# A fused perceiver block: value copies, one gather and the last query tile change their engine or their place

## The reference

```python
# ctx_1024: (16, 1601, 512); 16 heads of 32
q = split_heads(layernorm(x) @ Wq); k = split_heads(ctx @ Wk); v = split_heads(ctx @ Wv)
attn = softmax(einsum('bhid,bhjd->bhij', q, k) * 32 ** -0.5)
x = x + merge_heads(einsum('bhij,bhjd->bhid', attn, v)) @ Wp + bp
x = x + self_attention(layernorm(x))
x = x + spikes(square(relu(layernorm(x) @ W_fc.T)) @ W_proj.T)
```

## Time and profile before

| | |
|---|---|
| timed runs | 1820.93, 1821.0, 1822.01 us; median 1821.0 |
| profiled execution | 1822.05 us, its span 1820.3 us |
| granted TensorE clock, mean | 0.999 of 2.4 GHz |
| TensorE busy | 1786.8 us, 98% of the span |
| VectorE / ScalarE / GpSimd busy | 1260.9 / 825.9 / 908.5 us |
| one turn of the batch loop | 88.7 us (first key tiles at 675.26 and 763.96) |

### The profile page before, as it was taken

How to read it: one execution, slowest core, us unless ns; L and a number is a source line. 1 busy time by engine, 2 the same in 40 slices (tenths; PEclk the granted TensorE clock), 3 DMA queues, 4 the chain that set the end, 5 groups by cost and what they waited for, 6 DMA issues and landing times. The chain is left out here.

```text
span 1820.3 us, 65817 instructions
## 1 busy us (share of the span) xinstructions
PE 1786.8 (98%) x28788; PEld 1560.4 (86%) x28788; DVE 1260.9 (69%) x1942; ACT 825.9 (45%) x982; POOL 908.5 (50%) x824
## 2 busy tenths in 40 slices
PE   9999999999999999999999999999999999999998
PEld 8979898979898989898989898988888877778887
DVE  6765959595959585868677777768686867574265
ACT  4534545453535454444444444444454534344332
POOL 0434646464647373837374646464655563444111
PEclk9999999999999999999999999999999999999999
DMA  7210202020202020202020110202020232123110
GB/s 260 118 40 3 83 4 83 3 83 3 83 3 83 3 83 3 83 3 83 8 79 22 64 50 37 71 15 80 6 80 5 75 97 85 25 84 106 44 59 24
DMA packets 43359, 101.20 MB, mean 56 GB/s; under 512 B 19120, under 2 KB 20656, under 8 KB 42960
## 3 DMA queue, kind: packets, MB, share of 16 engines
q1 hardware_dynamic: 43088, 96.88, 15.2%
HBM read 86.48 MB, written 8.29 MB: 52 GB/s over the span
## 5 line engine op out<-in xcount | busy, mean ns | idle before, releaser
L556 POOL TENSOR_TENSOR fold<-fold,prob 128x256 f32<-128x256 f32 x698 | 695.5, 996 | 55.2
L114 PE MATMUL ring<-y_parts,w_keep 128*128 128x402 f32 (+1 forms) x3072 | 592.5, 349 | 16.0 <-DVE v_sb L719 14.5
L114 PEld LDWEIGHTS ring<-y_parts,w_keep 128*128 128x128 f32 x3072 | 554.5, 188 | 30.6 <-DVE v_sb L719 19.0
L114 PE MATMUL ring<-wv_s,y_parts 128*128 128x512 f32 x2304 | 549.4, 396 | 0.0
L114 PEld LDWEIGHTS ring<-wv_s,y_parts 128*128 128x128 f32 x2304 | 429.4, 188 | 98.4
L550 POOL TENSOR_TENSOR fold<-prob 128x256 f32<-128x256 f32 x64 | 100.7, 1573 | 626.0 <-ACT prob L610 626.0
L579 ACT ACTIVATE k_sb<-ring 128x402 f32<-128x402 f32 (+1 forms) x256 | 129.5, 506 | 414.7 <-PE ring L114 414.6
L747 DVE TENSOR_TENSOR fold<-fold,prob 128x512 f32<-128x512 f32 x192 | 185.4, 966 | 141.9 <-ACT prob L604 136.3
L604 ACT ACTIVATE prob<-s_ps 128x1536 f32<-128x1536 f32 (+1 forms) x128 | 199.9, 1562 | 132.6 <-PE s_ps L939 132.6
L785 DVE TENSOR_TENSOR prob<-prob,peak_rows 128x1024 f32<-128x1024 f32 (+1 forms) x192 | 248.2, 1347 | 2.2
L610 ACT ACTIVATE prob<-prob 128x1024 f32<-128x1024 f32 (+1 forms) x192 | 211.4, 1125 | 60.0 <-DVE prob L785 57.6
(11 more groups left out here) (214 smaller groups left out, 1569.5 us busy)
## 6 DMA issues: line engine op xcount, KB each, us to landing
y_raw<-yT SPq DMA_DIRECT2D x48, 804.0 KB, 6.1
y_raw<-yT SPq DMA_DIRECT2D x16, 792.0 KB, 9.7
f_raw<-w_ffn SPq DMA_DIRECT2D x22, 512.0 KB, 3.6
v_sb<-y_left SPq DMA_DIRECT2D x1, 2304.0 KB, 10.8
v_sb<-v_left SPq DMA_DIRECT2D x16, 130.0 KB
p_x<-x SPq DMA_DIRECT2D x4, 512.0 KB, 6.3
q_scratch<-p_x SPq DMA_DIRECT2D x8, 256.0 KB, 2.1
q_sb<-q_scratch SPq DMA_DIRECT2D x16, 128.0 KB, 2.6
```

The lines of the kernel that those rows point to most:

```text
L114: mm = pe.matmul(out, left(a, c), right(b, c), start=(c == 0 and n == 0), stop=(c == DC - 1 and n == 2))
L556: pool.tensor_tensor(acc[0:m], acc[0:m], prob[0:m, i, t, :], ALU.add).then_inc(sum_step, 1)
```

## The change

1. ScalarE copies all 12 value tiles of a batch, VectorE none. One semaphore (`ring_act_out`) now counts all copies out of the ring, and `emptied` waits for it alone. ScalarE's order in `values_phase` is written anew; in the loop the exponentials of block 3 stand between value tiles 7 and 10.
2. In the last batch, VectorE's `gather(0)` stands in front of `subtract(b, 3)`, and ScalarE's `gather(0)` and `gather(1)` and all value copies stand in front of the exponentials of block 3. VectorE's low part of the late weights moves behind `output(B - 1, 1)`.
3. The last of the eight query tiles is copied by ScalarE (`last_queries`) and stored by SyncE in the cross attention's block instead of the prologue's, through a free part of `k_sb`.

```diff
-ACT_N = KEYS + VT // 2
-DVE_N = VT - VT // 2
+ACT_N = KEYS + VT
...
+        self.last_q = self.k_sb[:, 1, 0:TT // 2 * P]
...
-            for n in range(NQ):
+            for n in range(NQ - 1):
                 half, i = half_of(n)
-                sp.wait_ge(q_ok, n + 1)
+                sp.wait_ge(sh.q_ok, n + 1)
                 sp.dma_start(q_dram[:, i, half * HT:(half + 1) * HT], xs[:, n]).then_inc(sh.q_out, 16)
...
             sp.dma_start(wv_raw, wv.rearrange("(c p) e -> p c e", p=P)).then_inc(wv_in, 16)
+            sp.wait_ge(sh.q_ok, 2 * NBLK)
+            sp.dma_start(q_dram[:, NBLK - 1, TOK // 2:], sh.last_q).then_inc(sh.q_out, 16)
             sp.wait_ge(sh.q_out, 16 * 2 * NBLK)
             load_q(0)
...
+            def last_queries():
+                act.wait_ge(sh.q_ps, 2 * NBLK)
+                act.activation(sh.last_q, s_ps[:, NBLK - 1, :], ACT.Copy).then_inc(sh.q_ok, 1)
+
             def keys_phase(b, past=True):
                 for c in range(KC):
                     key(b, 0, c)
                 if not past:
                     value_weights()
+                    act.wait_ge(sh.q_out, 16 * 2 * NBLK)
                 key(b, 1, 0)
...
                 if more:
                     high(b + 1, 1)
+                    exponential(b, 3, 0)
+                    value(b, 8)
+                    exponential(b, 3, 1)
+                    value(b, 9)
+                    exponential(b, 3, 2)
+                    high(b + 1, 2)
+                    value(b, 10)
+                    value(b, 11)
+                    high(b + 1, 3)
                 else:
                     gather(0)
-                exponential(b, 3, 0)
-                exponential(b, 3, 1)
-                value(b, 9)
-                exponential(b, 3, 2)
-                if more:
-                    high(b + 1, 2)
-                else:
+                    value(b, 8)
+                    value(b, 9)
                     gather(1)
-                value(b, 11)
-                if more:
-                    high(b + 1, 3)
-                else:
+                    value(b, 10)
+                    value(b, 11)
+                    exponential(b, 3, 0)
+                    exponential(b, 3, 1)
+                    exponential(b, 3, 2)
                     gather(2)
...
-                subtract(b, 3)
-                value(b, 8)
                 if more:
+                    subtract(b, 3)
                     low(b + 1, 0)
                     low(b + 1, 1)
+                    low(b + 1, 2)
+                    low(b + 1, 3)
                 else:
...
                     gather(0)
-                value(b, 10)
-                if more:
-                    low(b + 1, 2)
-                if more:
-                    low(b + 1, 3)
-                else:
+                    subtract(b, 3)
                     gather(1)
...
-                if u >= KEYS and (u - KEYS) % 2 == 0:
-                    reached(pe, dve_out, DVE_N * b + (u - KEYS) // 2 + 1)
-                elif u >= KEYS:
-                    reached(pe, act_out, ACT_N * b + KEYS + (u - KEYS) // 2 + 1)
-                else:
-                    reached(pe, act_out, ACT_N * b + u + 1)
+                reached(pe, act_out, ACT_N * b + u + 1)
```

More of the change, by code:

```diff
@@ L183, in __init__ @@
         self.y_hi_ok, self.y_lo_ok = sem("y_hi_ok"), sem("y_lo_ok")
-        self.q_out = sem("q_out")
+        self.q_out, self.q_ps, self.q_ok = sem("q_out"), sem("p_q_ps"), sem("p_q_ok")
+        self.last_q = self.k_sb[:, 1, 0:TT // 2 * P]
 def prologue(nc, x, yT, wq, wk, q_dram, sh, ident, ones, s_ps):
@@ L213, in prologue @@
         turned, xt_hi, xt_lo = sem("p_turned"), sem("p_xt_hi"), sem("p_xt_lo")
-        q_ps, q_ok, wq_hi, wq_lo, wk_hi = sem("p_q_ps"), sem("p_q_ok"), sem("p_wq_hi"), sem("p_wq_lo"), sem("p_wk_hi")
+        wq_hi, wq_lo, wk_hi = sem("p_wq_hi"), sem("p_wq_lo"), sem("p_wk_hi")
         block = ctx.enter_context(nc.Block())
@@ L318, in query @@
             def query(n):
-                act.wait_ge(q_ps, n + 1)
-                act.activation(xs[:, n, :], q_bank[n % 4], ACT.Copy).then_inc(q_ok, 1)
+                act.wait_ge(sh.q_ps, n + 1)
+                act.activation(xs[:, n, :], q_bank[n % 4], ACT.Copy).then_inc(sh.q_ok, 1)
             def context_high(q):
@@ L341, in _ @@
                     context_high(n - NBLK + 1)
-                query(n)
+                if n < NQ - 1:
+                    query(n)
         @block.tensor
@@ L374, in first_queries @@
                         mm = product(n, c, 0, 1, stop=(c == DC - 1))
-                    mm.then_inc(q_ps, 1)
+                    mm.then_inc(sh.q_ps, 1)
             def queries(units):
@@ L381, in queries @@
                     if n >= 4:
-                        pe.wait_ge(q_ok, n - 3)
+                        pe.wait_ge(sh.q_ok, n - 3)
                     three_passes(pe, q_bank[n % 4], lambda a, c: wq_s[:, a, c, i * P:(i + 1) * P],
-                                 lambda a, c: xnT[:, a, c, half * HT:(half + 1) * HT]).then_inc(q_ps, 1)
+                                 lambda a, c: xnT[:, a, c, half * HT:(half + 1) * HT]).then_inc(sh.q_ps, 1)
             pe.wait_ge(ident_ok, 2)
@@ L424, in cross_attention @@
         small_ps = ctx.enter_context(nc.psum_tensor("small_ps", [P, 512], F32))
-        full, act_out, dve_out = sem("ring_full"), sem("ring_act_out"), sem("ring_dve_out")
+        full, act_out = sem("ring_full"), sem("ring_act_out")
         q_in, s_full, s_out = sem("q_in"), sem("s_full"), sem("s_out")
@@ L581, in value @@
             def value(b, t):
-                if t == 1:
+                if t == 0:
                     reached(act, pv_ok, NBLK * b)
@@ L664, in values_phase @@
             def values_phase(b, more):
+                value(b, 0)
                 score(b, 2, 1)
                 value(b, 1)
+                value(b, 2)
                 score(b, 3, 0)
@@ L670, in values_phase @@
                 exponential(b, 2, 1)
+                value(b, 4)
                 score(b, 3, 1)
@@ L678, in values_phase @@
                     act.activation(y.keep[:, 0], y.w_raw, ACT.Copy).then_inc(wp_hi, 1)
+                value(b, 6)
                 value(b, 7)
@@ L681, in values_phase @@
                     high(b + 1, 1)
+                    exponential(b, 3, 0)
[7 more added lines that the diff above has]
+                    high(b + 1, 3)
                 else:
                     gather(0)
[L684 to L695 removed]
+                    value(b, 8)
+                    value(b, 9)
+                    gather(1)
+                    value(b, 10)
[3 more added lines that the diff above has]
+                    exponential(b, 3, 2)
                     gather(2)
+            last_queries()
             keys_phase(0, False)
@@ L712, in _ @@
         def _(dve):
[L713 to L719, removed]
             def left_low(j):
@@ L833, in keys_phase @@
                             left_low(j + LEFT_SLOTS)
-                value(b, 0)
                 if past:
@@ L840, in values_phase @@
                 largest(b, 2, 1)
-                value(b, 2)
                 row_of_peaks(b, 2)
                 subtract(b, 2)
-                value(b, 4)
                 largest(b, 3, 0)
                 largest(b, 3, 1)
-                value(b, 6)
                 row_of_peaks(b, 3)
-                subtract(b, 3)
-                value(b, 8)
                 if more:
+                    subtract(b, 3)
                     low(b + 1, 0)
                     low(b + 1, 1)
+                    low(b + 1, 2)
+                    low(b + 1, 3)
                 else:
@@ L876, in _ @@
             output(B - 1, 0, last_bank(0), q_sb[:, 0, :])
+            output(B - 1, 1, last_bank(1), q_sb[:, 1, :])
             dve.wait_ge(aw_hi, 1)
             dve.tensor_tensor(y.w_side[0][:, 1], sh.w_late[:], y.w_side[0][:, 0].bitcast(F32), ALU.subtract)
-            output(B - 1, 1, last_bank(1), q_sb[:, 1, :])
             output(B - 1, 2, last_bank(2), q_sb[:, 2, :])
@@ L951, in weigh @@
                     pe.wait_ge(act_out, ACT_N * (b + 1))
-                    pe.wait_ge(dve_out, DVE_N * (b + 1))
                     pe.wait_ge(v_in, 16 * (b + 1))
```

## The result

The changed kernel takes 1803.4 us in the median of 6 runs (1801.5 to 1804.9), the kernel before 1821.0 (1820.7 to 1822.0, 6 runs): ratio 0.9902, interval 0.9889 to 0.9915. The forecast was 1809.8 with a range of 1806 to 1814. The gain is 17.6 us where 11.2 were forecast, so the direction was right and the size wrong. The profiled execution of the changed kernel took 1802.7 us, with a span of 1800.9 against 1820.3.

The account below looks back on a forecast made before the run. TensorE was taken as the bound, with only its idle time to win: 8.1 + 1.1 (loop) + 1.1 (last queries) + 0.9 (last batch) = 11.2 us, so 1821.0 - 11.2 = 1809.8 us, range 1806 to 1814.

Parts of the forecast that it names:

- What bounds the kernel: Whole kernel: TensorE is busy 1786.8 of 1820.3 us, so only its idle time can be won.
- A second wait under the first, the branch: Batch loop's turn: under the wait for tile 10's copy lies TensorE's taken branch, 3602 ns, ending at 763.1.
- Restart behind the branch: Loop's turn: 0.24 us from the branch's end to the first key tile's weight load, bounds 0.16 to 0.53.
- rival 1: Loop's turn: all of the wait comes back because the branch's fetch shortens or starts earlier; 16.5 us, 1804.5, chance 0.10.
- Size of a stop: Loop's turn: TensorE idles 1.03 us between the last value matmul and the next batch's first key tile.
- the forecast's own case: Loop: branch still sets the key tile, idle 0.41 instead of 1.03 us; 8.1 us over 13 turns, 1.1 at the last.
- The gap in the loop: Loop: the gain from shorter TensorE stops between batches, 8.1 us in 13 turns plus 1.1 from batch 14 to 15.
- Last queries: Barrier after the prologue: read out in the next stage, the first key tile starts at 36.92 instead of 38.06; 1.1 us.
- Last batch: First output product: VectorE's earlier gather of quarter 0 removes TensorE's stop, 0.9 us; GpSimd's later work close, but hidden.
- ScalarE late: Loop's turn: in-order ScalarE copies tile 10 too late and the kernel gets slower, 1835 us in the example; chance 0.04.
- Rival 2: Loop's branch: another wait fills the gap, only 3.1 us come back, 1817.9, or half way, 1814; chance 0.12.

Follow-up runs that it names:

- e1: Kernel before, with VectorE's copy of value tile 10 moved in front of the low parts, tile 8 still copied late: 1812.1 us, ratio 0.9948.
- e4: Changed kernel, with ScalarE's copies of value tiles 8 and 9 moved behind the third exponential and the third high part: 1832.8 us, ratio 1.0054.
- e6: Changed kernel, with ScalarE's three exponentials first, then value tiles 8, 9 and 10, then the third high part: 1812.5 us, ratio 0.9950.
- e7: Kernel before, with only value tiles 8 and 10 given to ScalarE, VectorE keeping 0, 2, 4 and 6: 1803.8 us, ratio 0.9906.
- e5: Kernel before, with only the once-run parts changed (last queries, last batch), value copies still shared: 1820.4 us against 1821.3, ratio 0.9997.
- e3: Kernel before, with VectorE copying tile 8 before the fourth subtraction and tile 10 before the low parts: 1811.3 us, ratio 0.9938.

## Why the forecast came out too small

- *What bounds the kernel*: right. The gain is TensorE's stops and nothing else; its matmuls are the same 28788.
- *A second wait under the first, the branch*: right, and shown by e1. With tile 10 in time and all else as before, the branch sets the key tile.
- *Restart behind the branch*: 0.24 us taken, 0.27 measured, in e1, e4 and e6 alike.
- *The step that failed* is in the argument against rival 1: "the queue ahead of it is as deep as before". The 3.44 us by which the branch was issued ahead were read as the depth of the queue. They were the end of tile 8's copy plus 0.21 us. The row of that copy in the kernel before:

```profile
758.60 0.68 DVE L719 COPY v_sb<-ring 128x512 f32<-128x512 f32 x1
```

  The copy ends at 759.28 and the branch starts at 759.49. VectorE's lateness held the queue at tile 11's wait and the branch behind it, so the copies that the change took away were the cause of the second wait too. The forecast had worked out that tile 8 would be copied earlier (758.9 at the worst), but used it for tile 11 alone and left the branch at 759.5. Freed, the branch starts 4.21 us ahead, and its 3.3 to 3.9 us are covered. Rival 1 named this outcome ("starts earlier") and 1804.5 us, at a chance of 0.10.
- *Size of a stop*: 1.03 us listed, but a turn is 1.30 us shorter without it (88.70 against 87.40). The listed idle time starts at the modelled end of a matmul, 0.39 us after its start, while the value matmuls follow each other at 19.73 / 84 = 0.23 us: 0.16 more. Behind a stop the first 24 key matmuls also take longer, 4.33 us from the first one's start to the next tile's instead of 4.21: 0.12 more. As some branches still show a little, the mean of 14 turns is 1.25 (1.21 in e7).
- *Size of the forecast's own case*: 0.62 us a turn and 9.2 for the loop; e1 gained 0.78 and 10.9. The modelled end does not explain this, as it cancels where a stop is left. The branches of e1 were shorter, 3.45 us in the mean against 3.62 before, which leaves 0.28 us idle instead of 0.41; all kernels lie between 3.3 and 3.9, so this is chance as far as is known.
- *The gap in the loop*, 17.4 against 9.2 us: 6.5 are the branch's earlier start (17.4 against e1's 10.9), the other 1.7 what e1 gained over its forecast.
- *Last queries*: 1.1 us forecast, 0.9 and 1.1 found in the traces of after and e5. The query load went out at 43.49 and the scores started on time.
- *Last batch*: 0.9 forecast, 1.0 to 1.1 found at the first output product. GpSimd's bias rows end at 1461.90 + 8.26 = 1470.16, ahead of the barrier. The forecast let the late exponentials push them by all of their 7.4 us. Against the first output product GpSimd's sums start 8.3 us later but take 5.5 us instead of 11.4, so the bias rows start only 2.1 us later; what shortened the sums was not tested. By time, both parts together are not told from nothing (e5).
- *ScalarE late*: not in the changed kernel, whose tile 10 is out 1.8 us before the value matmuls end. The price of this rival was not tested on tile 10. e4 tests it on tile 8: there a few microseconds of order turn the gain into a loss.
- *Rival 2, another wait*: not there, but e3 shows one of its kind, VectorE's low part, at 0.45 us a turn.

## What to carry to other kernels

A time in the trace by which an instruction is issued early is not a property of the queue until one knows what it was waiting for: look at which semaphore wait stands in front of it and whether the engine that is late already also releases that one. When one late engine is relieved, recompute every event that follows from it, the second wait as well as the first. And when a change moves much work, try its smallest part: here two copies of six, in the right place of the order, gave all of it that the times can tell.

## What the runs showed of the hardware

- TensorE's taken loop branch costs 3.3 to 3.9 us in its queue, and little or nothing in time if it is issued 4.2 us before the queued matmuls run out. Where nothing is queued any more, the next matmul starts 0.27 us behind its end. A semaphore wait ahead of it in the queue holds it back: it then starts 0.21 us after the end of the copy that releases the wait (before, e1, e4, e6).
- 4.21 us ahead was the earliest start in all kernels. The longest branches still cost a little: the changed kernel has three of over 3.8 us in a row, and the four turns that they end or begin take 87.45 to 87.66 us, against 87.4.
- The start of the first key tile lay between 37 and 41 us from one profiled execution to another, with up to 2.8 us of waiting for ScalarE's transposed rows in the prologue. That is more than either of the once-only parts is worth.
